# Cross attention in a six-layer decoder kernel: the scaling of the probabilities on GpSimd instead of VectorE

## The chip, the cores and the metric

The kernel runs on one core of one Trainium2 chip. The metric is the device time in microseconds (us) of one execution of the whole program. Profiles are of one execution each; engines are named PE (TensorE matmuls), PEld (TensorE weight loads), DVE (VectorE), ACT (ScalarE), POOL (GpSimd) and SP (the engine that only issues transfers).

## The reference

Two decoder layers over x (4 batches, 512 rows, width 512) with a layer norm after each part: linear attention, a selective scan over the context, a squared-ReLU network with ternary weights, causal attention across the batch axis, cross attention, and a gated network whose weights are looked up in a 16-entry table. All is float32. The change touches the cross attention (x is `hidden_states`, the context has 512 rows of width 256, H = 16 heads of D = 128):

```python
q = rmsnorm((hidden_states @ Wq).reshape(B, Sq, H, D), gq)
k = rmsnorm((encoder_hidden_states @ Wk).reshape(B, Skv, H, D), gk)
v = (encoder_hidden_states @ Wv).reshape(B, Skv, H, D)
scores = jnp.einsum('bqhd,bkhd->bhqk', q, k) * scale
attn = jax.nn.softmax(scores, axis=-1)
out = jnp.einsum('bhqk,bkhd->bqhd', attn, v).reshape(B, Sq, H * D)
return out @ Wo
```

## The kernel before

Each engine has its own instruction list, written out by hand, and runs it in order; engines wait for one another through semaphores. Cross attention is stage 3 of the list of stages. It loops over the 4 batches `c` and the 16 heads `hh`; a head's 512 query rows are 4 tiles `t` of 128 rows, so that one tile of scores or probabilities is 128 x 512.

For one head the work goes round all the engines:

- PE computes the four score tiles into banks 4 to 7 (`scores`), then the queries of the next head, the weighted values of the head before (`weighted`, line 694), the transposed keys of the next head (line 1090), the sums of squares of its queries (`query_squares`, line 1097), in heads 1, 5 and 9 the values of the next group of four heads, and only then `turn_weights` (line 1115): 16 transposes of this head's probabilities, from p4 into a ring of three banks. In heads 2, 6 and 10 the keys of the next group follow (`keys`). Then comes the next head's `scores`.
- DVE takes each score tile's row maximum (line 2194) and turns it into a bias (line 2198). In heads 3, 7 and 11 it then scales the next group's keys (`key_scale`, line 2136). Then, tile by tile, it takes the reciprocal of the row sum (line 2205) and multiplies the probabilities by it in place (line 2207). Next it computes the low part of the next head's queries (`q_rest`, line 2146), of its keys (`k_rest`, line 2150) and the mean square of its queries (line 2142). Between these and behind them it decodes the last layer's weights from the table (`masks`, `first_pair` and so on: lines 2050 to 2065), which fills most of the rest of its time. In batch 0 it also splits weights (`wxq_rest`, line 2154, at the end of a head).
- ACT computes exp of a score tile into p4 and its row sum into sm4 (line 1554), then the squares and the high part of the next queries, copies the attended values, the keys (`turned_keys`) and their high part `k_hi` (line 1549), and the four transposed probability tiles pT.
- POOL does only small work here: the inverse roots for queries and keys (`query_rms`, lines 2401 and 2404; `key_rms`, line 2396).

`turn_weights` waits until all four tiles of the head are scaled, and its first bank is the one that the next head's queries were in, so that it also waits for `q_rest`:

```python
def turn_weights(c, hh):
    pe.wait_ge(p_ready, START + after(c, 4 * XH, 4 * hh + 4))
    for k in range(NT):
        d = bank4(c, "pT", hh, k)
```

The scaling before, on DVE, within its loop over tiles:

```python
dve.wait_ge(p_exp, START + after(c, 4 * XH, n + 1))
dve.reciprocal(sm4[:, 12 + t:13 + t], sm4[:, 8 + t:9 + t]).then_inc(rs_ready, 1)
dve.wait_ge(rs_ready, START + after(c, 4 * XH, n + 1))
dve.tensor_scalar(p4[:, t, :], p4[:, t, :], sm4[:, 12 + t:13 + t], None, ALU.mult).then_inc(p_ready, 1)
```

Of the kernel before, what the change touches and what calls it, by code (L numbers as in the profile page):

```python
# [21 lines left out]
ALU = mybir.AluOpType  # L22
# [6 lines left out]
NT = S // P  # L29
# [11 lines left out]
XH, XD = 16, 128  # L41
# [16 lines left out]
START = 1  # L58
# [3 lines left out]
def after(c, per, k):  # L62

    return c * per + k
# [21 lines left out]
def build(nc, io, stages=5):  # L86
# [7 lines left out]
    with ExitStack() as ctx:  # L94
        sems = []

        def sem(name):
            sems.append(ctx.enter_context(nc.semaphore(name)))
            return sems[-1]
# [157 lines left out]
        def hold(eng):  # L257

            eng.sem_inc(passed, 1)
# [140 lines left out]
        p4 = s4("p4", [P, NT, S])  # L400
        w_hi3 = Space(nc, s4.at)("w_hi3", [P, 2, D], F32R); w_lo3 = Space(nc, s4.at + 2 * 4 * D)("w_lo3", [P, 2, D], F32R)
        pT = s4("pT", [P, NT, S])
        sm4 = s4("sm4", [P, 16])
# [28 lines left out]
        rs_ready = sem("rs_ready"); p_ready = sem("p_ready")  # L432
# [1267 lines left out]
        def _(dve):  # L1700
# [335 lines left out]
            if stages >= 4:  # L2036
# [78 lines left out]
                for c in range(B):  # L2115
                    for p in (c % 2,):
# [15 lines left out]
                        def key_scale(c, g):  # L2132
                            for t in range(NT):
                                dve.wait_ge(k_pow, START + after(c, 16, 4 * g + t + 1))
                                v = kt4[:, t, :].rearrange("p (n d) -> p n d", d=XD)
                                dve.tensor_tensor(v, v, kss[:, t, :].rearrange("p (n a) -> p n a", a=1).to_broadcast([P, 4, XD]),
                                                  ALU.mult).then_inc(k_scaled, 1)
# [6 lines left out]
                        def q_rest(c, hh):  # L2144
                            dve.wait_ge(a_done, evicted4(c, "q", hh))
                            dve.tensor_tensor(q_lo[:, :], bank[TILES4[c, "q", hh] % 3][:, :], q_hi[:, :], ALU.subtract).then_inc(q_split, 1)  # L2146
# [43 lines left out]
                        for hh in range(XH):  # L2190
                            for t in range(NT):
                                n = 4 * hh + t
                                dve.wait_ge(v_full, START + V0[3] + after(c, PER_V[3], n + 1))
                                dve.tensor_reduce(sm4[:, t:t + 1], bank[4 + t][:, :], AX.X, ALU.max).then_inc(max_ready, 1)  # L2194
                                if t == 0:
                                    dve.wait_ge(rq_pow, START + after(c, XH, hh + 1))
                                dve.wait_ge(max_ready, START + after(c, 4 * XH, n + 1))
                                dve.scalar_tensor_tensor(sm4[:, 4 + t:5 + t], sm4[:, t:t + 1], -1.0, rq[:, hh % 2, 1, t:t + 1],  # L2198
                                                         ALU.mult, ALU.mult).then_inc(nmax_ready, 1)
                            if hh % 4 == 3 and hh < XH - 1:  # L2200
                                key_scale(c, hh // 4 + 1)
                            for t in range(NT):
                                n = 4 * hh + t
                                dve.wait_ge(p_exp, START + after(c, 4 * XH, n + 1))
                                dve.reciprocal(sm4[:, 12 + t:13 + t], sm4[:, 8 + t:9 + t]).then_inc(rs_ready, 1)
                                dve.wait_ge(rs_ready, START + after(c, 4 * XH, n + 1))
                                dve.tensor_scalar(p4[:, t, :], p4[:, t, :], sm4[:, 12 + t:13 + t], None, ALU.mult).then_inc(p_ready, 1)  # L2207
                            g, n, two = hh // 4, FIRST[c] + sum(LUTS[c][:hh // 4]), LUTS[c][hh // 4] == 2
                            if hh + 1 < XH:
                                q_rest(c, hh + 1)  # L2210
                            if hh % 4 == 0:
                                masks(n)
                            if hh % 4 == 2 and two:
                                second_pair(n + 1)
                            if hh + 1 < XH:
                                k_rest(c, hh + 1)
                                query_mean(c, hh + 1)
                            if hh % 4 == 0:
                                first_pair(n)
                                second_pair(n)  # L2220
                            if hh % 4 == 1:
                                third_pair(n)
                                fourth_pair(n)
                            if hh % 4 == 1 and two:
                                masks(n + 1)
                                first_pair(n + 1)
                            if hh % 4 == 2 and two:
                                third_pair(n + 1)
                            if hh % 4 == 3 and two:
                                fourth_pair(n + 1)  # L2230
                            if c == 0 and hh % 4 == 0 and hh // 4 + 1 < GROUPS:
                                wxv_rest(hh // 4 + 1)
                            if c == 0 and hh % 4 == 1 and hh // 4 + 1 < GROUPS:
                                wxk_rest(hh // 4 + 1)
                            if c == 0 and hh + 2 < XH:
                                wxq_rest(hh + 2)
                            if hh % 4 == 2 and hh // 4 < 3:
                                key_norms(c, hh // 4 + 1, range(NT))
                            if hh == 12 and c + 1 < B:
                                ctx_rest(c + 1)  # L2240
                        if c < B - 1:
                            n = FIRST[c] + sum(LUTS[c])
# [53 lines left out]
        def _(pool):  # L2296
# [96 lines left out]
            def key_rms(c, g):  # L2393
                for t in range(NT):
                    pool.wait_ge(k_mean, START + after(c, 16, 4 * g + t + 1))
                    pool.tensor_tensor(kss[:, t, :], kss[:, t, :], mhalf[:, 0:4], ALU.pow).then_inc(k_pow, 1)

            def query_rms(c, hh):
# [4 lines left out]
                hold(pool)  # L2403
                pool.tensor_scalar(r[:, 1, :], r[:, 0, :], float(XD) ** -0.5, None, ALU.mult).then_inc(rq_pow, 1)

            def cross(c):

                if c == 0:
                    key_rms(0, 0)
                    query_rms(0, 0)  # L2410
                for hh in range(XH):
                    if hh:
                        query_rms(c, hh)
                    if hh % 4 == 3 and hh < XH - 1:
                        key_rms(c, hh // 4 + 1)
                if c + 1 < B:
                    key_rms(c + 1, 0)
                    query_rms(c + 1, 0)
                for t in range(NT):
                    ln_pool(pool, T0[3] + after(c, PER_T[3], t), t % 2)  # L2420
                store_chunk(3, c)

            for n in range(1, min(stages, 5)):
# [8 lines left out]
                with pool.Fori(0, B // 2) as i:  # L2432
                    for p in range(2):
                        c = 2 * i + p
# [43 lines left out]
```

## Time and profile before

| | |
|---|---|
| Time, median of 3 runs | 2836.32 us (2829.55 to 2836.57) |
| The profiled execution | 2836.43 us, of which the trace spans 2834.7 us |
| Busy over the span | PE 91%, PEld 60%, DVE 72%, ACT 43%, POOL 25% |
| Mean granted TensorE clock | 0.954 of full speed |
| Heads of the cross attention | from about 1181 us to 2365 us, four batches with an output projection between them |

Busy shares are of the whole span. A PE that is busy all the time is not necessarily at its peak, since the ends of matmuls are modelled. Idle time of an engine that no one waits for costs nothing.

### The profile page before, as it was taken

The numbers are of one execution on the slowest core, as the hardware profiler recorded it, in microseconds if no ns is written. First come the engines' busy times: TensorE is split into PE (matmuls) and PEld (weight loads), VectorE is DVE, ScalarE is ACT, GpSimd is POOL, SyncE is SP. The second block draws the span as 40 slices with busy tenths as digits, with TensorE's granted clock in tenths as the row PEclk, the third lists the DMA queues.
The fourth block names the chain that finished last, engine by engine and source line by source line (L and its number), as shares of the span: only waits on it lengthen the run. The fifth ranks groups of instructions, "written<-read, shape, count | busy, mean of one in ns | idle before, by whom it ended". The sixth has DMA issues, their size and how long they took to land. (4 is left out here: it accounts for less than half of the span.)

```text
span 2834.7 us, 29502 instructions
## 1 busy us (share of the span) xinstructions
PE 2579.2 (91%) x9938; PEld 1707.4 (60%) x9938; DVE 2044.9 (72%) x3585; ACT 1207.1 (43%) x2171; POOL 705.2 (25%) x617
## 2 busy tenths in 40 slices
PE   6998898989789789789899999999999997999997
PEld 2343433434367555566667776777777774588886
DVE  3879999899975377687868897889878895231332
ACT  3453544634433221356554555465645564021111
POOL 1445445456401156211111220111111110000000
PEclk8989999999989899899999999999999998999999
DMA  4111211112311202322323223322323215100000
GB/s 147 52 46 61 67 65 61 53 37 74 113 58 40 87 30 75 119 100 102 130 71 114 77 79 108 123 75 86 105 71 120 82 46 172 60 9 22 31 15 15
DMA packets 81568, 212.47 MB, mean 75 GB/s; under 512 B 8966, under 2 KB 17414, under 8 KB 77324
## 3 DMA queue, kind: packets, MB, share of 16 engines
q1 hardware_dynamic: 72108, 178.25, 19.0%
q0 software_dynamic: 5472, 21.01, 1.9%
q10 hardware_dynamic: 3840, 11.34, 1.1%
q8 instruction: 80, 1.31, 0.2%
q14 instruction: 68, 0.56, 0.1%
HBM read 164.11 MB, written 46.47 MB: 74 GB/s over the span
## 5 line engine op out<-in xcount | busy, mean ns | idle before, releaser
L2327 POOL TENSOR_TENSOR h<-du,Bb 128x1024 f32<-128x1024 f32 x128 | 312.7, 2445 | 242.6 <-DVE h L1785 240.5
L1780 DVE TENSOR_TENSOR_SCAN h<-bank,h 128x512 f32<-128x512 f32 x256 | 300.0, 1208 | 39.7 <-ACT bank L1366 32.2
L1366 ACT ACTIVATE bank<-dt,A 128x512 f32<-128x512 f32 x256 | 175.6, 690 | 317.8 <-DVE h L1780 317.1
L1554 ACT ACTIVATE p<-bank,sm,rq 128x512 f32<-128x512 f32 x256 | 199.1, 778 | 223.6 <-DVE sm L2198 223.6
L2401 POOL TENSOR_TENSOR rq<-rq,mhalf 128x4 f32<-128x4 f32 x64 | 79.4, 1241 | 819.1 <-DVE rq L2142 819.1
L694 PE MATMUL bank<-pT,v 128*128 128x512 f32 x512 | 231.2, 594 | 0.8 <-ACT pT L1257 0.8
L279 POOL TENSOR_SCALAR rstd<-mv 128x1 f32<-128x1 f32 x96 | 29.9, 312 | 788.2 <-DVE mv L273 788.2
L908 PE MATMUL bank<-h,ident 128*128 128x512 f32 x256 | 148.6, 664 | 53.9 <-DVE h L1785 53.5
L2281 DVE TENSOR_TENSOR h<-bank,sg 128x512 f32<-128x512 f32 (+1 forms) x44 | 30.4, 690 | 228.5 <-PE bank L1205 228.5
L1034 PE MATMUL bank<-x_hi,wxq_s 128*128 128x512 f32 x512 | 169.9, 414 | 23.7 <-DVE wxq_s L2154 22.0
L2194 DVE TENSOR_REDUCE sm<-bank 128x1 f32<-128x512 f32 x256 | 175.0, 684 | 7.6 <-PE bank L1034 7.4
L1785 DVE TENSOR_TENSOR h<-h,Cb 128x1024 f32<-128x1024 f32 x128 | 175.3, 1370 | 7.0 <-DVE h L1780 0.5
L1115 PE MATMUL bank<-ident,p 128*128 128x128 f32 x1024 | 145.0, 299 | 23.9 <-DVE q_lo L2146 18.6
L2065 DVE COPY_PREDICATED val<-msk,val 128x516 f32<-128x516 int32 x192 | 144.4, 752 | 29.3 <-DVE val L2058 2.0
L694 PEld LDWEIGHTS bank<-pT,v 128*128 128x128 f32 x512 | 98.0, 192 | 99.5 <-issue 92.4
L1115 PEld LDWEIGHTS bank<-ident,p 128*128 128x128 f32 x1024 | 127.9, 156 | 34.2 <-DVE p L2207 20.5
L1257 ACT ACTIVATE pT<-bank 128x512 f32<-128x512 f32 x256 | 135.0, 601 | 30.8 <-PE bank L1115 30.6
L909 PE MATMUL bank<-h,ident 128*128 128x512 f32 x256 | 140.8, 634 | 0.0
L2207 DVE TENSOR_SCALAR p<-p,sm 128x512 f32<-128x512 f32 x256 | 124.5, 486 | 9.1
L1034 PEld LDWEIGHTS bank<-x_hi,wxq_s 128*128 128x128 f32 x512 | 100.5, 198 | 50.9 <-DVE wxq_s L2154 26.3
L2058 DVE TENSOR_SCALAR val<-msk,lx,le 128x516 uint32<-128x516 uint32 x256 | 128.3, 544 | 2.1
L1681 ACT ACTIVATE sg<-bank 128x512 f32<-128x512 f32 (+1 forms) x44 | 26.2, 595 | 213.2 <-PE bank L1205 213.2
(248 smaller groups left out, 6081.8 us busy)
## 6 DMA issues: line engine op xcount, KB each, us to landing
wxq_s<-wq_dram SPq DMA_DIRECT2D x48, 512.0 KB, 4.0
Bb<-bc_dram SPq DMA_DIRECT2D x32, 512.0 KB, 3.7
Cb<-bc_dram SPq DMA_DIRECT2D x32, 512.0 KB, 3.7
x_dram<-xo POOLq DMA_DIRECT2D x16, 1024.0 KB, 4.9
xc<-x_dram SPq DMA_DIRECT2D x16, 1024.0 KB, 5.3
woh<-in_Wo SPq DMA_DIRECT2D x64, 256.0 KB, 2.7
wxv_s<-wkv_dram SPq DMA_DIRECT2D x12, 1024.0 KB, 4.9
wxk_s<-wkv_dram SPq DMA_DIRECT2D x12, 1024.0 KB, 8.1
```

The source lines that it names most:

```text
L694: m = pe.matmul(dst, l, r, start=(k == 0), stop=(k == len(pairs) - 1))
L908: pe.matmul(bank[4 + et][:, :], ident[:, :], h[:, G % HR, 0, :], start=False, stop=False)
L909: pe.matmul(bank[4 + et][:, :], ident[:, :], h[:, G % HR, 1, :], start=False, stop=(w == NW - 1))\
L1034: m = pe.matmul(dst, l, r, start=(n == 0), stop=(n == len(pairs) - 1))
L1115: m = pe.transpose(d[:, t * P:(t + 1) * P], p4[:, t, k * P:(k + 1) * P], ident[:, :])
L1366: act.activation(bank[2 + n][:, :], dt[:, c % 2, et, :], ACT.Exp, scale=A[:, et, 2 * w + n:2 * w + n + 1]).then_inc(dA_ready, 1)
L1554: act.activation(p4[:, t, :], bank[4 + t][:, :], ACT.Exp, bias=sm4[:, 4 + t:5 + t], scale=rq[:, hh % 2, 1, t:t + 1], accum_out=sm4[:, 8 + ...
L1780: dve.tensor_tensor_scan(h[:, s, n, :], bank[2 + n][:, :], h[:, s, n, :], 0.0, ALU.mult, ALU.add).then_inc(scanned, 1)
L1785: dve.tensor_tensor(h[:, s, :, :], h[:, s, :, :], Cb[:, w % 2, :, :], ALU.mult).then_inc(hC_ready, 1)
L2065: dve.copy_predicated(val[:, s, :], m, val[:, other, :]).then_inc(lut_step, 1)
L2194: dve.tensor_reduce(sm4[:, t:t + 1], bank[4 + t][:, :], AX.X, ALU.max).then_inc(max_ready, 1)
L2327: pool.tensor_tensor(h[:, G % HR, :, :], du[:, et:et + 1, :].to_broadcast([P, 2, S]), Bb[:, w % 2, :, :], ALU.mult).then_inc(dBu_ready, 1)
```

## The change

The multiplication of a probability tile by its reciprocal leaves DVE's list and enters POOL's, with the same operands. DVE keeps the reciprocals; before each it waits until POOL has scaled the same tile of the head before, whose reciprocal lies in the same column of sm4. POOL scales a head's four tiles behind that head's `query_rms` (and, in heads 3, 7 and 11, `key_rms`), and ahead of the next head's. PE's wait is unchanged: all four tiles scaled.

```diff
                                 dve.wait_ge(p_exp, START + after(c, 4 * XH, n + 1))
+                                dve.wait_ge(p_ready, START + after(c, 4 * XH, max(0, n - 3)))
                                 dve.reciprocal(sm4[:, 12 + t:13 + t], sm4[:, 8 + t:9 + t]).then_inc(rs_ready, 1)
-                                dve.wait_ge(rs_ready, START + after(c, 4 * XH, n + 1))
-                                dve.tensor_scalar(p4[:, t, :], p4[:, t, :], sm4[:, 12 + t:13 + t], None, ALU.mult).then_inc(p_ready, 1)
...
+            def scale_weights(c, hh):
+                for t in range(NT):
+                    pool.wait_ge(rs_ready, START + after(c, 4 * XH, 4 * hh + t + 1))
+                    hold(pool)
+                    pool.tensor_scalar(p4[:, t, :], p4[:, t, :], sm4[:, 12 + t:13 + t], None, ALU.mult).then_inc(p_ready, 1)
...
                     if hh % 4 == 3 and hh < XH - 1:
                         key_rms(c, hh // 4 + 1)
+                    scale_weights(c, hh)
```

`hold` increments a semaphore (`passed`) on whose value no wait depends.

## Rows read from the trace of the kernel before

**Rows 1.** The page: span, and busy us (share of the span) of each engine.

```profile
span 2834.7 us, 29502 instructions
PE 2579.2 (91%) x9938; PEld 1707.4 (60%) x9938; DVE 2044.9 (72%) x3585; ACT 1207.1 (43%) x2171; POOL 705.2 (25%) x617
```

**Rows 2.** Busy time by stretch, batch 2: PE, PEld, DVE, ACT, POOL, granted clock.

```profile
1780.00:2080.00 300.00, 289.97 (x1357) 221.38 (x1356) 252.52 (x571) 169.88 (x341) 49.66 (x57) 0.98 0.28 94
```

**Rows 3.** Waits from 1185 to 2380 us: total us, times, longest.

```profile
DVE k_lo L2150 <- ACT k_hi L1549: 57.4, 34, 5.3
...
PEld bank L1115 <- DVE p L2207: 20.5, 13, 1.7
PE bank L1115 <- DVE q_lo L2146: 18.6, 12, 1.6
```

**Rows 4.** DVE in order of time, batch 2, heads 8 to 11: start us, us.

```profile
1951.65 0.68 DVE L2194 TENSOR_REDUCE sm<-bank 128x1 f32<-128x512 f32 x1
...
1960.50 0.69 DVE L2150 TENSOR_TENSOR k_lo<-kr,k_hi 128x512 fp32r<-128x512 f32 x1 [1.06 <-ACT k_hi L1549]
...
1982.54 0.68 DVE L2194 TENSOR_REDUCE sm<-bank 128x1 f32<-128x512 f32 x1
...
1985.78 0.16 DVE L2205 RECIPROCAL sm<-sm 128x1 f32<-128x1 f32 x1
...
1988.16 0.68 DVE L2146 TENSOR_TENSOR q_lo<-bank,q_hi 128x512 fp32r<-128x512 f32 x1
1988.76 1.00 DVE L2058 TENSOR_SCALAR val<-msk,lx,le 128x516 uint32<-128x516 uint32 x2
...
2000.20 0.68 DVE L2194 TENSOR_REDUCE sm<-bank 128x1 f32<-128x512 f32 x1
...
2005.86 0.16 DVE L2205 RECIPROCAL sm<-sm 128x1 f32<-128x1 f32 x1
...
2008.23 0.68 DVE L2146 TENSOR_TENSOR q_lo<-bank,q_hi 128x512 fp32r<-128x512 f32 x1
2008.83 0.68 DVE L2150 TENSOR_TENSOR k_lo<-kr,k_hi 128x512 fp32r<-128x512 f32 x1
```

**Rows 5.** ACT in order of time, the last exp tile of head 10.

```profile
1985.90 0.78 ACT L1554 ACTIVATE p<-bank,sm,rq 128x512 f32<-128x512 f32 x1
```

**Rows 6.** PE in order of time, transposes of heads 8, 10 and 11.

```profile
1959.65 2.02 PE L1115 MATMUL bank<-ident,p 128*128 128x128 f32 x16
...
1989.70 2.02 PE L1115 MATMUL bank<-ident,p 128*128 128x128 f32 x16
...
2009.06 1.97 PE L1115 MATMUL bank<-ident,p 128*128 128x128 f32 x16 [1.52 <-DVE q_lo L2146]
```

**Rows 7.** PE and DVE in order of time, batch 2, head 0.

```profile
1833.75 3.32 PE L1115 MATMUL bank<-ident,p 128*128 128x128 f32 x16
...
1827.57 0.68 DVE L2194 TENSOR_REDUCE sm<-bank 128x1 f32<-128x512 f32 x1
```

**Rows 8.** PE and DVE in order of time, batch 3, head 15.

```profile
2362.55 2.00 PE L1115 MATMUL bank<-ident,p 128*128 128x128 f32 x16 [0.34 <-DVE p L2207]
...
2356.77 0.69 DVE L2194 TENSOR_REDUCE sm<-bank 128x1 f32<-128x512 f32 x1 [0.29 <-PE bank L1034]
```

**Rows 9.** Groups by line and form: busy us, mean ns of one, idle before.

```profile
L2327 POOL TENSOR_TENSOR h<-du,Bb 128x1024 f32<-128x1024 f32 x128 | 312.7, 2445 | 242.6 <-DVE h L1785 240.5 <-PE bank L909 1.3 <-DMA Bb<-bc_dram 0.8
...
L2358 POOL TENSOR_TENSOR prod<-qkv 128x512 f32<-128x512 f32 x40 | 53.7, 1364 | 35.3 <-ACT qkv L1257 31.5 <-DVE sc L1964 3.7
...
L279 POOL TENSOR_SCALAR rstd<-mv 128x1 f32<-128x1 f32 x96 | 29.9, 312 | 788.2 <-DVE mv L273 788.2
...
L2207 DVE TENSOR_SCALAR p<-p,sm 128x512 f32<-128x512 f32 x256 | 124.5, 486 | 9.1
```

**Rows 10.** DVE and POOL in order of time, where both work in SBUF.

```profile
1013.42 1.74 DVE L1997 TENSOR_TENSOR at<-at,pv 128x512 f32<-128x512 f32 x1 [0.96 <-POOL pv L2367]
...
1013.36 1.26 POOL L2358 TENSOR_TENSOR prod<-qkv 128x512 f32<-128x512 f32 x1
```

## The prediction

> **What bounds the kernel now.** I read the page first: PE is busy 91% of the span and POOL 25%, so DVE with 72% is the second engine, not the first [rows 1]. The share by stretch says it more sharply for the heads: in batch 2 PE is busy 290 of 300 us at a granted clock of 0.98, DVE 253 and POOL 50 [rows 2]. The order in time then shows why DVE's 16% of idle time is not PE's: PE runs from one head into the next and the only regular hole is ahead of the transposes of heads 3, 7 and 11, 1.52 us long, where PE waits for `q_lo` [rows 6]. The list of waits has 18.6 us of this kind in 12 heads, one each [rows 3]. So in this stretch PE sets the pace, and DVE matters only where PE waits for it.
>
> For each head I measure from the start of its first row maximum on DVE, and call that zero. Two times decide: when the last probability tile is scaled, and when PE comes to the transposes.
>
> - Heads 0, 4, 8, 12: PE comes at 8.0 in head 8 (1951.65 and 1959.65) [rows 4, 6], and within 0.4 us of that or later in heads 4 and 12. In head 0 of batches 1 to 3 it comes at 6.2 (1827.57 and 1833.75) [rows 7].
> - Heads 1, 5, 9: the values of the next group lie ahead of the transposes on PE; it comes some 5.5 us later than in the others.
> - Heads 2, 6, 10: PE comes at 7.2 in head 10 (1982.54 and 1989.70) [rows 4, 6]; in head 2 it is 6.9.
> - Heads 3, 7, 11: `key_scale` pushes the reciprocals back. They begin at 5.7 (2000.20 and 2005.86) in place of 3.2 (1982.54 and 1985.78) [rows 4]. PE is there at 7.3 (9.06 less the hole of 1.52, both from 2000) and starts at 8.9 [rows 6].
>
> Four tiles on DVE take 2.4 us from the first reciprocal to `q_lo` (1985.78 to 1988.16, 2005.86 to 2008.23) [rows 4], so all are scaled at 5.7 to 5.8 in a normal head and 8.1 in heads 3, 7 and 11: mostly ahead of PE, by 1.3 to 2.3 us in heads 8 and 10.
>
> **What is removed.** 256 instructions of 486 ns, 124.5 us of DVE time [rows 9]. What is it worth? The last reciprocal of a head still needs the last exp, which ends 4.1 after zero (1985.90 + 0.78) [rows 5], so `q_lo` begins at about 4.35 in place of 5.6, and at about 6.0 in place of 8.0 in heads 3, 7 and 11. Behind `q_lo` stands `k_lo`, and that does not come sooner: it waits for ACT's `k_hi`, as in head 8, 1.06 us [rows 4], 57.4 us in 34 heads [rows 3]. ACT gets its keys from PE's own order. The table decoding and the next head's first maximum hang on `k_lo`. So most of the 1.3 to 2 us that DVE wins in each head become idle time ahead of `k_lo`, and I cost the removal at nothing for the heads' pace. Only the hole of heads 3, 7 and 11 would close, if the scaled tiles were there in time. If the cover were gone (PE no longer the bound), DVE's saving could be worth up to 1.3 us per head.
>
> **What is added.** Four instructions in a row on POOL per head, and the trace has no one-input POOL instruction of this size. Nearest rows [rows 9]: a two-input POOL product takes 1364 ns at 512 elements and 2445 at 1024, that is 2.11 ns per element for two inputs. Half of that for one input is 0.54 us for 512, and the small one-input instruction (1 element) costs 312 ns, together 0.85 us. The bound above is the two-input instruction, 1.36 us; the bound below is DVE's own 0.49. I take 0.85, as it has the right fixed cost and one stream in place of two, and 0.05 between two of them: 0.9 per tile.
>
> To this comes contention. A two-input DVE instruction of 128x512 takes 0.68 us in the heads [rows 4] but 1.74 when it starts just behind a POOL instruction of 1.26 [rows 10]: it waited for POOL to end and then ran. The Trainium skill (SBUF — State Buffer, "Who interferes with whom") says that the pair of ports which GpSimd shares with VectorE is an exclusive lock, held for the whole instruction, for GpSimd against VectorE's two-port modes and its instructions with two SBUF inputs; the pair of rows agrees. I use it both ways: behind `q_lo` (one of its inputs is in PSUM, and I let it pass) DVE has the masks in heads 0, 4, 8, 12 and the table entries of 0.5 us each in heads 2, 6, 10 (1.00 for two) [rows 4]. One or two of these get in between POOL's tiles: 0.8 to 1.0 us more for POOL.
>
> POOL starts 0.1 us behind the first reciprocal, at 3.5. All tiles are scaled at 3.5 + 4 x 0.9 = 7.1 without contention, about 7.9 in heads 0, 4, 8, 12 and 8.1 in heads 2, 6, 10. In heads 3, 7, 11 POOL starts at 5.9 and meets `k_lo`: 9.5 without it, 9.7 with a part of its 0.68. Against PE's times above:
>
> - Head 0, batches 1 to 3: 7.9 less 6.2, 1.7 each; batch 0 (PE comes at 6.9) 1.0. Sum 6.
> - Heads 2, 6, 10 of batches 1 to 3: 8.1 less 6.9 to 7.2, about 1.0 each, nine times. Sum 9. In batch 0 PE comes at 10 in two of them; 0.4 once.
> - Heads 3, 7, 11, all batches: 9.7 less 8.9, 0.85, twelve times. Sum 10.
> - Head 14 of batches 1 and 3, in which tables are decoded as in head 10: 1.2 each. Sum 2.4.
> - Head 15, batch 3: PE starts at 5.8 now and waits for the last tile even so [rows 8]; with table work behind the reciprocals POOL ends at 8.2: 2.4. Batch 1: 0.8. Sum 3.
> - Heads 1, 5, 9, 4, 8, 12: nothing. Head 13: 0.5, but PE waits in head 14 anyway, which takes it up.
>
> Together 31 us. A wait of PE at the transposes delays the next scores, queries and keys, and PE has no later hole for it in batches 1 to 3. In batch 0 PE also waits for split weights, and I take off 1 us there: +30 us. The profiled execution took 2836.4 us (2834.7 of span and 1.7 around it), the same as the median of the runs, so the forecast is 2866 us.
>
> The other costs are small. DVE's new wait for the tile of the head before is over long before, 10 us earlier. Behind the four tiles on POOL stands the next head's `query_rms`, which was started 9.4 to 9.6 after zero and now can be 0.3 us late; DVE needs it at the next head's first bias, 2 us later, and behind that DVE instruction are the maxima and ACT's exps. In heads 1, 5, 9 POOL is done before. `key_rms` stays ahead of the tiles, so `key_scale` is not touched. No DMA and no order on SP changes.
>
> The price per tile has the greatest leverage: 0.1 us more makes the last tile 0.4 later in some 30 heads, 10 to 13 us in all.
>
> **The rivals.**
>
> *A tile costs POOL like a two-input instruction, 1.26 to 1.36 us* [rows 9, 10]. Then all are scaled at 9.5 and in heads 3, 7, 11 at 11.1: head 0 some 12 us, heads 2, 6, 10 some 23, heads 3, 7, 11 some 27, heads 14 and 15 some 11, batch 0's other heads 3: +76, 2912 us. For it: no POOL row of this size is faster than 1 us. Against it: those rows read two streams.
>
> *A tile costs no more than a one-input DVE instruction at its plain rate, 0.68 us* (the row maxima [rows 4]). Then the tiles are ready at 7.1 in heads 2, 6, 10, as PE comes, and at 8.7 in heads 3, 7, 11, 0.15 ahead of today. What stays is head 0 and the last one, 4 us, less 2: 2838 us, no change. The Trainium skill is on this side: GPSIMD Engine Reference, "Engine selection", calls one-input work roughly line-rate, and its section on elementwise cost gives 769 ns for 512 elements in a plain loop. An estimate with 0.77 from that page would be +16, 2852 us; no row here can show it.
>
> *Faster.* If a tile took 0.49 us on POOL, as on DVE, the tiles of heads 3, 7 and 11 would be ready at 5.9 + 4 x 0.49 = 7.9, `q_lo` at 6.6, and PE would start at 7.9 in place of 8.9: 12 times 1.0, 2824 us. This decides below 0.6 us per tile. The hole is there [rows 6], the price has no row for it.
>
> **How the numbers follow.** Forecast case (0.77 to 1.1 us per tile, 2850 to 2890 us) 0.56; two-input price 0.20; no change 0.17; faster 0.07. About 0.3%, 8.5 us, is what a measurement of this kernel can tell from no change. Slower 0.76, same 0.17, faster 0.07. The range reaches down to the no-change case, 2838, and up halfway to the two-input case, 2905; outside are the faster case, half of the no-change case and the worse half of the two-input case.
>
> **What the profile of the changed kernel would show.** The POOL instructions on p: 0.85 us each, median, some 0.4 longer where DVE's masks or table entries come between. DVE's busy time down by some 120 us, less what its two-input and table instructions grow by. DVE idle ahead of `k_lo` longer than 57 us. PE's wait ahead of the transposes for POOL, about 30 times, some 50 us in all with the 18.6 of `q_lo` gone into it, and heads 1, 5, 9 without one. The heads of batch 2 some 7 us longer in all. Wrong would be: a tile price below 0.7 or above 1.1; or POOL instructions that hold DVE so long that the table decoding, not the transposes, is late, which would show as first maxima that come later after PE's scores than today.

## The result and the profile after

| | before | after |
|---|---|---|
| median of the runs, us | 2832.94 (4 runs, same chip) | 3003.18 (4 runs) |
| spread, us | 2824.17 to 2836.57 | 2996.45 to 3012.59 |
| ratio, 95% interval | | 1.0616 (1.0589 to 1.0643) |
| span of the profiled execution, us | 2834.7 | 2994.7 |

The change makes the kernel 170 us slower. Forecast were 30 us, with 2905 as the upper end of the range. The direction and the place were right, the size was not. In two of the kernels below one run was in a slower state, 77% and 14% longer than the others, and it is left out of their times and ratios.

The page of the changed kernel, first its totals by engine, then lines of the costliest groups (busy us, mean ns of one | idle us before it, and what ended the idle time); they answer to [rows 1, 9]:

```profile
span 2994.7 us, 30014 instructions
...
PE 2606.8 (87%) x9938; PEld 1745.9 (58%) x9938; DVE 1986.0 (66%) x3329; ACT 1219.2 (41%) x2171; POOL 1132.1 (38%) x873
...
L2409 POOL TENSOR_SCALAR p<-p,sm 128x512 f32<-128x512 f32 x256 | 427.5, 1687 | 442.2 <-DVE sm L2206 442.2
...
L1115 PE MATMUL bank<-ident,p 128*128 128x128 f32 x1024 | 180.2, 348 | 170.6 <-POOL p L2409 170.0
...
L2058 DVE TENSOR_SCALAR val<-msk,lx,le 128x516 uint32<-128x516 uint32 x256 | 154.2, 644 | 2.1
```

The first group line holds the result: a tile costs POOL 1687 ns, not 900. The second shows where it lands: PE sat idle for 170.6 us ahead of the transposes, against 23.9 us before, and the transposes themselves take 180.2 us, against 145.0. That is 147 and 35 us, together 182; the span grew by 160, so the rest of the kernel gave some 22 us back. The third line is a side effect of the change: VectorE's 256 table instructions, which nobody edited, went from 128.3 to 154.2 us.

The shortest, median and longest of POOL's tiles, from the view of everything that touches `p`:

```profile
L2409 POOL TENSOR_SCALAR p<-p,sm x256: 1556/1566/2529, 1173.4 to 2521.1; 128x512 f32<-128x512 f32 x128
```

The plain price is 1.56 us: 156 of the 256 tiles take at most 1.60. The other 100 raise the mean, up to 2.53 us, and most of them overlap VectorE's table work.

The list of waits over the heads (us in total, times, longest), to be read beside [rows 3]:

```profile
PEld bank L1115 <- POOL p L2409: 172.0, 50, 5.8
PE bank L1115 <- POOL p L2409: 166.0, 50, 5.6
...
DVE k_lo L2150 <- ACT k_hi L1549: 92.5, 45, 5.2
...
DVE sm L2194 <- PE bank L1034: 65.9, 24, 6.3
...
DVE q_lo L2146 <- ACT q_hi L1257: 53.3, 47, 2.2
```

PE waits for POOL 50 times where some 30 were forecast, and 3.3 us each time where 1.7 us were. The three rows below it show that the lighter VectorE gained nothing: it waits longer for ACT's `k_hi` (57.4 us before) and `q_hi` (4.6 before), and for PE's scores (6.4 before).

One head in order of time, head 11 of batch 2 (its wait of 5.57 us is the longest; 5.2 is usual in heads 3, 7 and 11 from batch 1 on), whose counterpart is in [rows 4, 6]. POOL, then PE (start us, us, and in brackets the idle time before):

```profile
2100.29 6.84 POOL L2409 TENSOR_SCALAR p<-p,sm 128x512 f32<-128x512 f32 x4 [4.84 <-DVE sm L2206]
...
2100.67 0.95 PE L1097 MATMUL bank<-ones,sq 128*128 128x1 f32 x8
2107.19 3.67 PE L1115 MATMUL bank<-ident,p 128*128 128x128 f32 x16 [5.57 <-POOL p L2409]
2110.51 0.78 PE L1034 MATMUL bank<-k_hi,q_hi 128*128 128x512 f32 x1
```

The head's first maximum is at 2094.27. PE is there 7.35 us after it, as in the kernel before (7.3 in the prediction), POOL is done at 12.86 and PE starts at 12.92. Then the same sixteen transposes take 3.67 us in place of 1.97. Windows laid over this stretch (PE, PEld, DVE, ACT, POOL busy us, then the granted clock; the last two numbers, of DMA, aren't used) say why:

```profile
2096.80:2101.60 4.80, 4.80 (x21) 2.77 (x19) 4.02 (x12) 3.86 (x10) 1.31 (x1) 1.00 0.00 0
2101.70:2107.10 5.40, 0.00 (x0) 0.00 (x0) 3.98 (x7) 0.60 (x1) 5.40 (x4) 0.91 0.00 2
2107.20:2110.50 3.30, 3.30 (x16) 3.30 (x17) 0.53 (x1) 1.65 (x3) 1.62 (x2) 0.50 0.47 111
2110.60:2112.80 2.20, 2.20 (x8) 1.72 (x7) 0.62 (x1) 0.64 (x2) 0.00 (x0) 0.50 1.00 345
2112.90:2117.20 4.30, 4.30 (x20) 3.52 (x19) 3.00 (x11) 3.33 (x8) 1.10 (x1) 0.99 1.06 432
```

PE runs at a granted 1.00, that is 2.4 GHz, does nothing for 5.4 us, comes back at a granted 0.50, that is 1.2 GHz, and stays there through the transposes and the first scores. So this wait is paid twice. The same holds for all 31 waits of more than 3 us: behind them the transposes take 3.3 to 3.7 us. In head 8, where PE waited only 0.84 us, they took 2.00; in head 10, behind 4.80, they took 3.56:

```profile
2047.68 2.00 PE L1115 MATMUL bank<-ident,p 128*128 128x128 f32 x16 [0.84 <-POOL p L2409]
...
2082.39 3.56 PE L1115 MATMUL bank<-ident,p 128*128 128x128 f32 x16 [4.80 <-POOL p L2409]
```

The length of the wait alone does not decide it. In the kernel before, PE waits 1.50 to 1.63 us in twelve heads; in eight of them the transposes take 1.97 us, as in [rows 6], in four 2.97 to 3.57, as here in head 3 of batch 3 (granted clock 0.53 from 2185.60 to 2189.20):

```profile
2185.59 3.57 PE L1115 MATMUL bank<-ident,p 128*128 128x128 f32 x16 [1.62 <-DVE q_lo L2146]
```

### The profile page after: what moved, and what is told of

The parts are those of the page before. It is cut to its first block and busy times, and to the rows that moved or that the text cites. A ratio compares the mean times of both kernels' runs of the same rounds, so it can differ in the third digit from the quotient of the medians.

```text
span 2994.7 us, 30014 instructions
## 1 busy us (share of the span) xinstructions
PE 2606.8 (87%) x9938; PEld 1745.9 (58%) x9938; DVE 1986.0 (66%) x3329; ACT 1219.2 (41%) x2171; POOL 1132.1 (38%) x873
## 5 line engine op out<-in xcount | busy, mean ns | idle before, releaser
L2409 POOL TENSOR_SCALAR p<-p,sm 128x512 f32<-128x512 f32 x256 | 427.5, 1687 | 442.2 <-DVE sm L2206 442.2
L1115 PE MATMUL bank<-ident,p 128*128 128x128 f32 x1024 | 180.2, 348 | 170.6 <-POOL p L2409 170.0
L1115 PEld LDWEIGHTS bank<-ident,p 128*128 128x128 f32 x1024 | 159.0, 182 | 181.2 <-POOL p L2409 176.0
L1257 ACT ACTIVATE pT<-bank 128x512 f32<-128x512 f32 x256 | 142.4, 602 | 204.1 <-PE bank L1115 203.7
L908 PE MATMUL bank<-h,ident 128*128 128x512 f32 x256 | 147.3, 658 | 53.7 <-DVE h L1785 53.1
L1034 PE MATMUL bank<-x_hi,wxq_s 128*128 128x512 f32 x512 | 165.8, 406 | 17.1 <-DVE wxq_s L2154 15.6
L2058 DVE TENSOR_SCALAR val<-msk,lx,le 128x516 uint32<-128x516 uint32 x256 | 154.2, 644 | 2.1
L2395 POOL TENSOR_TENSOR kss<-kss,mhalf 128x4 f32<-128x4 f32 x64 | 82.2, 1284 | 160.4 <-DVE kss L2130 155.7
```

The costliest lines, as they stand in the source:

```text
L1034: m = pe.matmul(dst, l, r, start=(n == 0), stop=(n == len(pairs) - 1))
L1115: m = pe.transpose(d[:, t * P:(t + 1) * P], p4[:, t, k * P:(k + 1) * P], ident[:, :])
L2058: dve.tensor_scalar(val[:, s, :].bitcast(U32), msk[:, 0, :].bitcast(U32), lx[:, j:j + 1], le[:, j:j + 1], ALU.bitwise_and, ALU.bitwise_xor ...
L2409: pool.tensor_scalar(p4[:, t, :], p4[:, t, :], sm4[:, 12 + t:13 + t], None, ALU.mult).then_inc(p_ready, 1)
```

## The experiments

The theory after the result: the whole loss comes from the time at which the last tile is scaled in each head. It has three parts: POOL's price, PE's clock behind the long waits, and contention between VectorE and POOL. The rivals: contention alone is what costs, or VectorE's lighter load matters more than was said. Below, a difference to the kernel before is taken from the ratio, one between two other kernels from their medians.

### What a tile costs POOL

Behind the last store of the kernel before, POOL runs a few instructions on dead memory, each waiting for the one before:

```diff
+ one(lambda: pool.tensor_scalar(a, a, s, None, ALU.mult))           # L2450; L2451 256, L2452 128 columns
+ one(lambda: pool.tensor_scalar(b, a, s, None, ALU.mult))           # L2453
+ one(lambda: pool.tensor_scalar(b, a, -0.5, None, ALU.mult))        # L2454
+ one(lambda: pool.tensor_tensor(b, a, s.to_broadcast([P, S]), ALU.mult))  # L2455
+ one(lambda: pool.tensor_tensor(b, a, b, ALU.mult))                 # L2456
+ one(lambda: pool.tensor_copy(b, a))                                # L2457
```

> The kernel before, and behind its last store POOL runs eight forms of instruction on dead memory, three times over, each waiting for the one before, with no DVE work beside them. Same output; the time itself says nothing. One tile as in the change (product with a per-row pointer, in place, 512 elements): 1.56 us, as its fastest in the changed kernel. If the price goes by element, with 0.23 us fixed: 0.90 us at 256 and 0.56 at 128 elements. If the pointer operand is what costs, the same product with a constant takes 0.8 us or less and the one that writes elsewhere takes 1.56; if the instruction itself costs, the constant takes 1.56 too. A two-input product should take 1.26 us, as in the row of the attention stage, a product with the row's reciprocal broadcast as second input 1.06 to 1.26.

POOL in order of time, the last round of them:

```profile
2856.60 1.56 POOL L2450 TENSOR_SCALAR rsum<-rsum,mhalf 128x512 f32<-128x512 f32 x1
2858.26 0.92 POOL L2451 TENSOR_SCALAR rsum<-rsum,mhalf 128x256 f32<-128x256 f32 x1
2859.28 0.60 POOL L2452 TENSOR_SCALAR rsum<-rsum,mhalf 128x128 f32<-128x128 f32 x1
2859.98 1.56 POOL L2453 TENSOR_SCALAR rsum<-rsum,mhalf 128x512 f32<-128x512 f32 x1
2861.63 1.49 POOL L2454 TENSOR_SCALAR rsum<-rsum 128x512 f32<-128x512 f32 x1
2863.20 1.04 POOL L2455 TENSOR_TENSOR rsum<-rsum,mhalf 128x512 f32<-128x512 f32 x1
2864.32 1.26 POOL L2456 TENSOR_TENSOR rsum<-rsum 128x512 f32<-128x512 f32 x1
2865.65 0.61 POOL L2457 COPY rsum<-rsum 128x512 f32<-128x512 f32 x1
```

With nothing beside it the instruction takes 1.56 us, so its price is not contention. With a constant in place of the column of scalars it is 1.49, and 1.56 with the result written elsewhere, so neither the column nor working in place is what costs. From 128 to 512 columns it grows by 0.96 us, 2.5 ns per element, on a base of 0.28. And it is dearer than the product of two full tiles (1.26), which the prediction had taken for the bound above. The same product with the reciprocal broadcast along the row as a second operand takes 1.04. A copy takes 0.61, so reading one stream is cheap on POOL; it is this operation that is not.

### The cheaper form in the change

```diff
- pool.tensor_scalar(p4[:, t, :], p4[:, t, :], sm4[:, 12 + t:13 + t], None, ALU.mult)
+ pool.tensor_tensor(p4[:, t, :], p4[:, t, :], sm4[:, 12 + t:13 + t].to_broadcast([P, S]), ALU.mult)
```

> The changed kernel, but POOL multiplies each tile by its reciprocals as the second input of a two-input product, broadcast along the row: 1.04 us by itself in place of 1.56. Same output. Theory (last tile late, price per tile sets it): four tiles end 2.1 us sooner, at about 8.5 in most heads and 10.3 in heads 3, 7 and 11; PE's holes shrink by 2 us each and most get too short to bring the clock down. By the sum on record with 1.09 per tile: +55 us, with some of the clock's cost +55 to +80, 2885 to 2910 us. Rival (it is POOL's share of the memory that costs, whatever the form): a two-input instruction holds the ports as well, and the time stays within 30 us of the change's 3003 us.

Measured: 2898.68 us, 1.0230 (1.0205 to 1.0255). The tiles, in the view of `p`:

```profile
L2409 POOL TENSOR_TENSOR p<-p,sm x256: 1028/1040/1579, 1182.4 to 2433.3; 128x512 f32<-128x512 f32 x128
```

The same work on the same engine takes 1.04 in place of 1.56 us, and some 105 us of the 170 are gone. 0.52 us per tile for 105 us is 20 us for each 0.1 us, where the prediction had said 10 to 13. A part of that is contention, which the new form meets less of: in head 10 of batch 2 the four tiles take 4.21 us, close to four times the price, where the change needs 7.45, and heads 4, 8 and 12 no longer wait.

The clock did not come back as expected. The transposes take 169.0 us in this kernel, against 145.0 before and 180.2 in the change. PE's waits are now at most 3.5 us, and behind all thirteen of 1.3 to 1.6 us the transposes are slow, 2.9 to 3.7 us. Head 0 of batch 2, with the window over its transposes:

```profile
1863.35 3.68 PE L1115 MATMUL bank<-ident,p 128*128 128x128 f32 x16 [1.56 <-POOL p L2409]
...
1863.40:1867.00 3.60, 3.60 (x17) 3.60 (x18) 3.42 (x9) 1.79 (x3) 1.60 (x2) 0.50 0.57 232
```

### Where it costs

The change for some heads alone, VectorE scaling in the others:

```diff
- for t in range(NT):
+ for t in [t for t in range(NT) if hh in (1, 5, 9)]:    # second kernel: hh in (3, 7, 11)
```

> POOL scales in heads 1, 5 and 9 alone, DVE in all others; same output. Theory (what costs is PE's wait for late tiles): in the changed kernel these 12 heads had their last tile at 9.8 to 10.2 us after the first maximum and PE came at 12.6 to 14.9, so there is no wait and the time is that of the kernel before within 0.3%. Rival (what costs is that POOL and DVE hold each other up, wherever PE stands): the 168 us fall on 64 heads alike, 2.6 us each, 12 heads 31 us, 1.1% slower.

> POOL scales in heads 3, 7 and 11 alone; same output. Theory with tile price and clock: the last tile comes at 12.4 us in place of 8.1 and PE starts at 12.5 in place of 8.9, 3.6 us in each of 12 heads, and the transposes behind a hole of 5 us take 3.6 us in place of 2.0 at a lower clock, 1.6 us more: 12 times 5.2, +62 us, about 2895 us. Late tiles alone, without the clock: 12 times 3.6, +43 us, 2876 us. Rival (cost spread over all heads alike): 12 times 2.6, +31 us, 2864 us.

Measured: heads 1, 5, 9: 2840.15 us, 1.0028 (1.0002 to 1.0055); heads 3, 7, 11: 2898.03 us, 1.0215 (1.0170 to 1.0260). As many tiles move to POOL in both. Where the values of the next group lie ahead of the transposes they cost some 8 us (interval 1 to 16), where PE is already early they cost 61 us, 5.1 us for each of twelve heads, as the theory said. The view of `p` in the second kernel has PE's and PEld's wait together:

```profile
  POOL p L2412: 126.5, 24
```

Twelve heads, two entries each: some 5.3 us of wait in place of 1.5. The remaining 1.3 us of the 5.1 fit the slower clock behind the wait.

### The clock behind the waits

The change again, but PE transposes the identity into the next bank, where it overwrites nothing of use, 32 to 42 times ahead of each long wait:

```diff
 def turn_weights(c, hh):
+    fill = {0: 32, 2: 34, 6: 36, 10: 36, 3: 42, 7: 42, 11: 42}.get(hh, 0) if c or hh % 4 == 3 else 0
+    d = bank4(c, "pT", hh, 0)
+    for _ in range(fill):
+        pe.transpose(d[:, 0:P], ident[:, :], ident[:, :])
     pe.wait_ge(p_ready, START + after(c, 4 * XH, 4 * hh + 4))
```

> The changed kernel, but PE turns the identity 32 to 42 times into the bank that it will use next, before it waits for the scaled tiles, in heads 3, 7 and 11 of all batches and 0, 2, 6 and 10 of batches 1 to 3 (24 heads). Same output; PE is busy in place of idle while POOL scales. Theory (behind a hole of 4 to 5 us the clock is at its lower level, transposes take 3.6 us in place of 2.0, and the next scores start slowly): 24 times 1.6 to 2.1 us come back, 40 to 50 us less than the change, about 2958 us. Rival (transposes are slow there for another reason, such as POOL's or ACT's work beside them): no gain, 3003 us or more.

Measured: 2962.11 us, 1.0449 (1.0420 to 1.0477), 41 us less than the change, with useless work added. PE in head 11 of batch 2:

```profile
2084.94 4.78 PE L1114 MATMUL bank<-ident 128*128 128x128 f32 x42
2090.67 2.00 PE L1119 MATMUL bank<-ident,p 128*128 128x128 f32 x16 [0.95 <-POOL p L2413]
2092.43 0.48 PE L1034 MATMUL bank<-k_hi,q_hi 128*128 128x512 f32 x1
```

The transposes start at the same distance from the first maximum as in the change and take 2.00 us again in place of 3.67. So some 41 of the 170 us (47 by the ratios) are the slower clock, not the wait. The Trainium skill (TensorE: Matmul & The Clock Gate, Part 1) says that the array's clock is halved when PE has lately been idle. The windows above agree, with 0.50 granted behind 5.4 us without work; the size, 1.7 us per head on the transposes, is from the rows here. When a wait of 1.3 to 1.6 us brings the clock down and when it doesn't stays open: the kernels here show both.

### Contention and VectorE's lighter load

First nobody scales: the reciprocal itself releases PE, and the division is left out of the result. Then the same with POOL's four instructions per head put beside it on scratch memory, waited for by no one.

```diff
- dve.reciprocal(...).then_inc(rs_ready, 1)
- dve.wait_ge(rs_ready, ...)
- dve.tensor_scalar(p4[:, t, :], p4[:, t, :], sm4[:, 12 + t:13 + t], None, ALU.mult).then_inc(p_ready, 1)
+ dve.reciprocal(...).then_inc(p_ready, 1)
# second kernel, POOL, per head and tile, also:
+ pool.tensor_scalar(scr[:, :], scr[:, :], mhalf[:, 1:2], None, ALU.mult).then_inc(timed, 1)
```

> Left out: the probabilities are not divided by their sum; each tile counts as scaled when DVE has its reciprocal, and POOL does nothing more than before. Theory (PE sets the pace, DVE's saving goes into its own wait ahead of k_lo): only the hole ahead of the transposes of heads 3, 7 and 11 closes, 12 times 1.5 us, so some 18 us under the kernel before, about 2815 us. Rival (DVE's time is itself worth something): 1.3 to 2 us in each of 64 heads, 80 to 125 us less, 2710 to 2750 us.

> Left out: the division of the probabilities, as in the run without scaling (2804 us). Added to it: POOL runs the change's four one-input products of 128x512 per head at the same points, but on a scratch tile and waited for by no engine. Theory (contention costs little, the wait is all): DVE's table instructions grow by some 30 us in sum, most of it ahead of k_lo, and the time is 2804 to 2815 us. Rival (contention on the shared memory path carries the loss): a good part of the 168 us appears, 2850 us or more.

Measured: no scaling 2803.91 us, 0.9886 (0.9845 to 0.9926); with POOL beside it 2849.14 us, 1.0057 (1.0039 to 1.0075). Two things were off. VectorE's work is worth more than the closed hole: about 32 us (interval 21 to 44), not 18. And POOL's unneeded instructions cost 45 us, where 11 at most was expected. The groups of VectorE by form, without and with them:

```profile
L2065 DVE COPY_PREDICATED val<-msk,val 128x516 f32<-128x516 int32 x192 | 144.4, 752 | 28.6 <-DVE val L2065 1.0
...
L2058 DVE TENSOR_SCALAR val<-msk,lx,le 128x516 uint32<-128x516 uint32 x256 | 128.2, 544 | 2.1
```

```profile
L2061 DVE TENSOR_SCALAR val<-msk,lx,le 128x516 uint32<-128x516 uint32 x256 | 159.0, 663 | 2.1
L2068 DVE COPY_PREDICATED val<-msk,val 128x516 f32<-128x516 int32 x192 | 154.3, 804 | 28.6 <-DVE val L2068 1.0
```

These two groups alone take 40.7 us more. PE doesn't wait for POOL at the transposes in that kernel, so the loss comes by other ways: PE waits 13.3 us for the keys that VectorE scales, and not at all without POOL's work, and 24.8 us for the queries' high part, 17.5 without it; VectorE waits 13.7 us ahead of its biases for POOL's query scale, which is queued behind the scratch work. In the change itself VectorE has room, 66 us of waiting for scores, so there this cost may be covered; no run here shows it apart.

The next experiment takes the contention out of the change: the masks and table entries that stood behind `q_lo` go behind `k_lo` and the query's mean.

```diff
-    if hh % 4 == 0: masks(n)
-    if hh % 4 == 2 and two: second_pair(n + 1)
     if hh + 1 < XH: k_rest(c, hh + 1); query_mean(c, hh + 1)
+    if hh % 4 == 0: masks(n)
+    if hh % 4 == 2 and two: second_pair(n + 1)
```

> The change, with VectorE's table masks (heads 0, 4, 8, 12) and table entries (heads 2, 6, 10) moved behind k_lo and the query's mean, so that they no longer run while GpSimd scales. Theory: the last tile of heads 2, 6 and 10 is ready at 9.8 in place of 11.1 us after the first maximum and that of heads 0, 4, 8 and 12 at 10.0 in place of 10.4; with 9 to 12 heads at 1.2 and as many at 0.4 that is 15 to 22 us less than the change, ratio to before about 1.054. Rival: VectorE's tables do not hold GpSimd up, only the other way round; then the last tiles come as in the change, and the time is within 5 us of it (ratio 1.060).

Measured: 3003.32 us, 1.0614 (1.0592 to 1.0635), the time of the change. Yet the tiles did come sooner. POOL in head 10 of batch 2, in the change and in this kernel:

```profile
2074.88 7.45 POOL L2409 TENSOR_SCALAR p<-p,sm 128x512 f32<-128x512 f32 x4 [10.29 <-DVE sm L2206]
```

```profile
2086.83 6.35 POOL L2409 TENSOR_SCALAR p<-p,sm 128x512 f32<-128x512 f32 x4 [8.94 <-DVE sm L2206]
```

Four tiles take 6.35 us in place of 7.45, and PE's wait for POOL fell from 166.0 to 147.3 us. The span did not fall. VectorE idles ahead of `k_lo` for longer (138.6 in place of 92.5 us) and does its tables later, and PE's other waits on VectorE and ACT grew by about as much as that for POOL fell: for `q_hi` from 5.2 to 15.7 us, for split weights from 15.6 to 21.8, for scaled keys from nothing to 4.2. So the mechanism of the theory held, and its saving was given back at other places.

### Sharing the tiles

POOL scales tile 0 of each head, VectorE the other three.

```diff
- for t in range(NT):
+ for t in [t for t in range(NT) if t == 0]:
```

> The change for tile 0 of each head alone; VectorE scales tiles 1 to 3. Theory: GpSimd has tile 0 from 3.5 to about 5.1 us after the first maximum, before VectorE has the last one, so PE waits nowhere for it; in heads 3, 7 and 11 VectorE is done 0.4 us earlier: 2826 to 2836, ratio 0.998 to 1.002. Rival: GpSimd's instruction keeps VectorE out of SBUF while it runs, the other three tiles come about 1 us later, and heads 3, 7, 11 and the first heads pay for it: 2842 to 2855, ratio 1.004 to 1.009.

Measured: 2829.01 us, 0.9997 (0.9986 to 1.0009): no difference, in the theory's band. But something of the rival's mechanism is there, in the view of `p`:

```profile
L2209 DVE TENSOR_SCALAR p<-p,sm x192: 485/724/848, 1172.5 to 2346.2; 128x512 f32<-128x512 f32 x192
L2412 POOL TENSOR_SCALAR p<-p,sm x64: 1564/1845/1867, 1172.5 to 2344.9; 128x512 f32<-128x512 f32 x64
```

Of VectorE's three tiles in a head the first takes 486 ns as before, the other two, beside POOL, some 724 and 775; POOL's takes 1845 ns at the median, not 1566. Neither engine is kept out for the other's whole instruction. From the first reciprocal to `q_lo` it is 2.42 us in head 10 of batch 2, and 2.38 in the kernel before [rows 4]: the quarter handed over is lost again on the other three.

### Other places for the division

ScalarE scales, behind the squares and the rounded query of the next head:

```diff
+ for t in range(NT):
+     act.wait_ge(rs_ready, START + after(c, 4 * XH, 4 * hh + t + 1))
+     act.activation(p4[:, t, :], p4[:, t, :], ACT.Copy, scale=sm4[:, 12 + t:13 + t]).then_inc(p_ready, 1)
```

> The kernel before, with ScalarE in place of VectorE scaling the probabilities, behind the squares and the rounded query of the next head. ScalarE's copy with a scale of 128x512 should be near 0.6 us. Theory: the tiles are ready at about 5.6 + 4 x 0.6 = 8.0, as PE comes in most heads, but k_hi, for which VectorE's k_lo waits, comes 2.4 us later, and so do PE's scores of the next head in some heads: 2840 to 2880, ratio 1.00 to 1.02. Rival 1: ScalarE has room enough ahead of k_hi and the time is that of the kernel without scaling, about 2805 (0.99). Rival 2: it costs as much as GpSimd, 2900 or more.

Measured: 2902.50 us, 1.0276 (1.0243 to 1.0309), in the second rival's band, though GpSimd's own figure is 100 us more. One tile is 721 ns at the median, less than half of POOL's, and PE waits for it only 38.9 us, but `k_hi` stands behind the four: VectorE's wait for it went from 57.4 to 158.8 us.

The second place is the transpose itself: VectorE scales the 128x128 identity, and PE multiplies by that diagonal.

```diff
- dve.tensor_scalar(p4[:, t, :], p4[:, t, :], sm4[:, 12 + t:13 + t], None, ALU.mult)
+ dve.tensor_scalar(diag[:, t, :], ident[:, :], sm4[:, 12 + t:13 + t], None, ALU.mult)
- pe.transpose(d[:, t * P:(t + 1) * P], p4[:, t, k * P:(k + 1) * P], ident[:, :])
+ pe.matmul(d[:, t * P:(t + 1) * P], p4[:, t, k * P:(k + 1) * P], diag[:, t, :], start=True, stop=True)
```

> Nobody scales the tiles: DVE multiplies the identity (128x128) by the reciprocals, one small instruction per tile, and PE's transposes become products with this diagonal, which scale as they turn. Same result. Theory (what bounds is when the last of DVE's four steps ends, and PE's work): a step is 128 elements in place of 512, 0.2 to 0.25 us; the last diagonal is ready at 4.7 and at 7.0 in heads 3, 7 and 11, so the time is near that of the run without scaling, 2804 to 2815 us, if a product over 128 columns takes PE 0.11 us as a transpose does (0.43 us for 512 columns in the weighted values). Rival (a product costs PE more than a transpose): 1024 of them at 0.1 us more are 100 us, 2930 us.

Measured: 2900.74 us, 1.0233 (1.0205 to 1.0262). The groups by line:

```profile
L1116 PE MATMUL bank<-diag,p 128*128 128x128 f32 x2048 | 253.8, 284 | 8.7 <-DVE q_lo L2147 8.7
...
L2208 DVE TENSOR_SCALAR diag<-ident,sm 128x128 f32<-128x128 f32 x256 | 73.4, 287 | 9.1
```

VectorE's part went down from 124.5 to 73.4 us, but 1024 transposes became 2048 instructions, 253.8 us in place of 145.0. A transpose of fp32 runs as one instruction here, a product of the same shape as two, so the condition of the theory, a product as cheap as a transpose, did not hold.

### The hole in heads 3, 7 and 11

A version meant to beat both: VectorE scales as before, and of the key scaling only the 128 columns of the next head stand ahead of the reciprocals; the other 384 go behind `k_lo`.

```diff
 if hh % 4 == 3 and hh < XH - 1:
-    key_scale(c, hh // 4 + 1)
+    key_scale(c, hh // 4 + 1)            # kt4[:, t, 0:128] alone
 ...
     k_rest(c, hh + 1)
     query_mean(c, hh + 1)
+if hh % 4 == 3 and hh < XH - 1:
+    key_scale_others(c, hh // 4 + 1)     # kt4[:, t, 128:512], its own semaphore for PE and ACT
```

> The kernel before, with VectorE still scaling the probabilities, and with the key scaling in heads 3, 7 and 11 split: ahead of the reciprocals only the 128 columns that the next head needs, the other 384 behind k_lo. Theory: the hole of 1.5 us ahead of the transposes in these heads is pure waiting of PE for VectorE's order, so moving some 1.6 us of work behind k_lo closes it: 12 holes, 15 to 18 us less than before, ratio about 0.994. Rival: the table work or the next head's maxima, pushed back by the same 1.6 us, become late, and the time stays within 5 us of before.

Measured: 2830.08 us, 0.9999 (0.9983 to 1.0015): no gain. The hole is gone: the list of waits no longer has PE waiting for `q_lo`, 18.6 us in [rows 3]. VectorE in order of time in head 11 of batch 2, from the key scaling to the first maximum of head 12:

```profile
2007.16 0.89 DVE L2137 TENSOR_TENSOR kt<-kt,kss 128x128 f32<-128x128 f32 x4
...
2011.99 0.69 DVE L2156 TENSOR_TENSOR k_lo<-kr,k_hi 128x512 fp32r<-128x512 f32 x1 [0.96 <-ACT k_hi L1550]
...
2012.68 1.96 DVE L2142 TENSOR_TENSOR kt<-kt,kss 128x384 f32<-128x384 f32 x4
2014.55 1.00 DVE L2059 TENSOR_SCALAR val<-msk,lx,le 128x516 uint32<-128x516 uint32 x2
...
2018.14 0.68 DVE L2201 TENSOR_REDUCE sm<-bank 128x1 f32<-128x512 f32 x1
```

`k_lo` comes no earlier than ACT allows, and from it on VectorE has no idle time ended by another engine up to the first maximum, whose scores PE had written by 2013.9. From one head's first maximum to the next it is 14.2 us here (2003.91 to 2018.14), 13.2 in the kernel before (2000.20 to 2013.43). Head 12 behind it is shorter by 0.8, and heads 11 and 12 together take 28.2 us, against 28.0. In heads 7 and 8 it is 27.1 and 26.9, and in both kernels VectorE waits there for another engine 1.0 to 1.1 us only: over such a pair VectorE's own list has next to no slack either. PE's hole and VectorE's backlog lay in the same head; closing the first moved the work into the second.

## Why the prediction was wrong in size

**The price of a tile is the step that failed.** It was worked out as "half of that for one input", 0.85 + 0.05 us, with "the bound above is the two-input instruction, 1.36 us". Measured alone it is 1.56 us; four in a row take 6.18 us in an undisturbed head and 6.84 in head 11 above. The argument scaled a price with the number of inputs, across two different operations. The runs show that on POOL it does not go that way: 0.61 for a copy, 1.04 and 1.26 for two operands, 1.56 for one operand and a scalar, at the same size. So the true price lay above the range's own bound, and the rival with the two-input price (2912 us) was too low as well. The Trainium skill's sentence on line-rate one-input work (GPSIMD Engine Reference, "Engine selection") agrees with the copy and not with the scaling; the estimate of 0.77 us, which came from another passage of that page, is half of what the scaling takes.

Where the waits fell, by the heads in which PE waits, in us added to the kernel before:

| heads | forecast | measured |
|---|---|---|
| 0 | 6 | 16 |
| 2, 6, 10 | 9 | 44 |
| 3, 7, 11 | 10 | 44 |
| 4, 8, 12 | 0 | 12 |
| 13 | 0 | 13 |
| 14 and 15 | 5 | 22 |

**The leverage, by the prediction's own rule.** 0.1 us per tile was to be 10 to 13 us. 1.56 + 0.05 less 0.9 is 0.71, so 71 to 92 us on top of the 30: 2937 to 2958 us, against 2962 of the kernel with filled waits, in which the clock mostly stays up. For the broadcast form (1.04 + 0.05) the same rule gives 2866 + 19 to 25, at most 2891, and 2899 was measured, with PE's long waits unfilled. So with the right price the scheme of arrival times gives most of the loss, 101 to 122 of 131 us and 49 to 55 of 68. That it comes so near is in part luck: between the two forms on POOL 0.1 us was worth 20, and the heads costed at nothing are missing in the sum. It names the classes of heads rightly for the most part: PE's arrivals at 7.35 and 6.3 in heads 11 and 10 are at most 0.9 us from those said, heads 1, 5, 9 have no wait, and heads 2, 6, 10 and 3, 7, 11 carry the most.

**A term was missing: PE's clock.** The prediction costs a wait at its length. Behind waits of 3.4 to 5.6 us the transposes and the first scores run at 1.2 GHz; filled waits give 41 us back. The term would not have been small at the forecast price either: the broadcast kernel, with waits of at most 3.5 us, still spends 24 us more on its transposes than the kernel before, where the change spends 35. The trace of the kernel before has the effect too, in four of its twelve waits of 1.5 to 1.6 us; the prediction shows one of the other eight [rows 6].

**Heads said to be free were not.** Heads 4, 8 and 12 were costed at nothing, as the tiles were to be there at 7.9 for PE's 8.0. They are scaled at 10.4 to 10.8, and PE, which now arrives at 9.5 to 10.05, waits about 1 us in each (head 8 of batch 2: 0.84 us). Head 13 was to be taken up by the wait of head 14; it waits 2.9 to 3.7 us, and head 14 waits as well. That is why PE waits 50 times, not 30.

**The removal at nothing was nearly right, but not for the reason given.** Of the 124.5 us removed from VectorE the kernel without scaling gets 32. The prediction allowed 18, the hole of heads 3, 7 and 11. The split of the key scaling shows that closing the hole by moving work behind it is worth nothing, since VectorE has a backlog there. Without the scaling, heads 7 and 8 of batch 2 take 25.2 us in place of 26.9, with PE busy throughout; twelve such pairs at 1.7 would be 20 us, an estimate from this one pair. So in these heads VectorE's list had next to no slack, which "in this stretch PE sets the pace" leaves out. In the change hardly any of it can arrive, as PE waits for POOL: VectorE's idle time ahead of `k_lo` grew from 57.4 to 92.5 us, as said, and its waiting for scores from 6.4 to 65.9.

**Contention** was put at 0.8 to 1.0 us for POOL in heads 0, 4, 8, 12 and 2, 6, 10. By the later-tables kernel it is 1.1 us in head 10 (7.45 less 6.35), but only some 0.6 in heads 4, 8 and 12, so the size was about right. The mechanism was not: from one pair of rows [rows 10] the prediction had VectorE's two-input instructions and POOL's shut each other out for a whole instruction. In the change `k_lo`, which reads two tiles in SBUF, starts in the middle of one of POOL's tiles in head 11 and takes 0.74 us in place of 0.68, without waiting for the tile's end (710 against 687 ns in the mean of all heads):

```profile
2102.33 0.74 DVE L2150 TENSOR_TENSOR k_lo<-kr,k_hi 128x512 fp32r<-128x512 f32 x1 [1.47 <-ACT k_hi L1549]
```

Instead both sides run slower. The tables themselves stretch, by 26 us in all, and in the kernel that shares the tiles VectorE's own scaling does.

Still open: the difference between the sum of the parts and the measured 170 us is not resolved by head, when a short wait brings PE's clock down, and why POOL's scaling by a scalar is dearer than its product with a broadcast operand.

## What to carry to other kernels

A price on another engine is taken from that operation at that size, measured alone; neither the number of its inputs nor a dearer-looking neighbour bounds it, and ten lines behind the last store measure it. When an engine that sets the pace gets a wait of several microseconds, cost the wait and the slower stretch behind it; here even some waits of 1.3 to 1.6 us had one. And a hole of the bounding engine is worth its length only if the next engine in the chain has no backlog in the same place: look at the distance between two heads' first maxima, not at the hole.

## What was not expected of the hardware

- On GpSimd, fp32, 128x512: product with a column of scalars 1.56 us, with a constant 1.49, product with the same column broadcast as a tensor 1.04, product of two tensors 1.26, copy 0.61. The same function in another instruction form saves a third of it, and 105 us in this kernel.
- VectorE's one-input scaling goes from 486 to between 724 and 848 ns beside GpSimd's, its integer table entries from 544 to 663 ns in the mean, and GpSimd's scaling from 1.56 to as much as 2.53 us: both sides lose.
- TensorE after 5.4 us without work: sixteen transposes in 3.67 us in place of 2.00, at a granted clock of 0.50. Behind a wait of 1.56 us they took 3.68 in one kernel; behind waits of 1.50 to 1.63 in another they took 1.97 eight times and 2.97 to 3.57 four times.
- A 128-column fp32 product with a diagonal runs as two instructions, where the transpose by the identity is one.
